# A decoder layer on one core: thresholds for each FFN matrix by itself, and all 16 tiles of FFN rows turned by transfers

## The reference

```
x = layernorm(x + latent_attention(x))         # 16 heads, 64 latent keys, softmax over the 4 largest
x = layernorm(x + cross_attention(x, ctx))     # 16 heads, low-rank keys and values from ctx, rope
x = layernorm(x + ffn(x))

# ffn, gains g1, g2, g3:
linear_bit(x, w, g) = act_quant(rmsnorm(x, g)) @ ternary(w).T
act_quant(x)        = round(x * 127 / max|x|) * max|x| / 127          # per row
ternary(w)          = round(tanh(w / s)) * arctanh(s),  s = mean|w|   # one s per matrix
h                   = silu(linear_bit(x, w1, g1)) * linear_bit(x, w2, g2)
ffn(x)              = linear_bit(h, w3, g3)                           # w1, w2: 1024 x 256, w3: 256 x 1024
```

## Time and profile before

| | us |
|---|---|
| three timed runs | 341.0, 341.74, 341.8 (median 341.74) |
| the profiled execution | 338.98 |
| its span, first to last instruction | 337.2 |
| mean granted TensorE clock | 0.993 of full speed |
| packets' data | 30.67 MB, 15.01 MB of it read from HBM |

### The profile page before, as it was taken

The page is one execution under the profiler, slowest core; times in us unless marked ns, Lnnn a source line. Parts: engine busy times, 40 slices in busy tenths (PEclk is TensorE's granted clock), DMA queues, the critical chain, the costliest instruction groups (busy, mean ns, idle before and its releaser), DMA issues.

```text
span 337.2 us, 7128 instructions
## 1 busy us (share of the span) xinstructions
PE 306.2 (91%) x2368; PEld 196.8 (58%) x2371; DVE 277.7 (82%) x704; ACT 279.7 (83%) x495; POOL 263.0 (78%) x282
## 2 busy tenths in 40 slices
PE   7788999989898979999999999999999999888882
PEld 3587678444576655564755658565757555555441
DVE  1397426999987799999998999998989999998861
ACT  2569889995468667777997979999899989999994
POOL 3265704889899994999996898999878999988641
PEclk9979999999999999999999999999999999999999
DMA  7999930005103120141030343528436235543011
GB/s 229 231 412 404 405 108 2 1 2 96 29 2 64 32 48 17 33 78 32 18 66 16 64 83 44 94 48 143 80 73 77 56 72 118 110 80 77 1 49 47
DMA packets 58292, 30.67 MB, mean 91 GB/s; under 512 B 53584, under 2 KB 56144, under 8 KB 57168
## 3 DMA queue, kind: packets, MB, share of 16 engines
q1 hardware_dynamic: 58256, 30.22, 36.7%
HBM read 15.01 MB, written 2.10 MB: 51 GB/s over the span
## 4 chain that ended last, share of the span: by engine, by line
PE 47%; ACT 16%; POOL 12%; issue 11%; DMA 7%; DVE 5%; SPq 0%; POOLq 0%; ACTq 0%; DVEq 0%
PE wide L575 10%; PE wide L607 6%; DMA region_c<-in_wkcqT 4%; PE wide L563 4%; PE wide L632 3%; POOL P L1419 3%; PE wide L538 3%; PE wide L495 3%; PE wide L531 3%; PE wide L589 2%; DMA w_raw<-w_raw 2%; ACT region_t L940 2%; PE wide L469 2%; ACT region_c L934 2%; PE wide L507 2%
## 5 line engine op out<-in xcount | busy, mean ns | idle before, releaser
L575 PE MATMUL wide<-B_sb,x1T 128*128 128x512 f32 x128 | 57.9, 597 | 0.8 <-DVE region_c L1218 0.8
L1111 DVE MAX8 m<-Ls 128x8 f32<-128x64 f32 x256 | 34.0, 209 | 14.9 <-ACT Ls L812 14.8
L607 PE MATMUL wide<-V,PT 128*128 128x256 f16 x384 | 44.7, 273 | 0.4 <-DVE V L1154 0.2
L607 PEld LDWEIGHTS wide<-V,PT 128*128 128x128 f16 x384 | 36.8, 98 | 8.9 <-issue 2.3
L1384 POOL TENSOR_TENSOR Ls<-Ls,m 128x1024 f32<-128x1024 f32 x16 | 30.9, 1932 | 10.7 <-DVE m L1111 10.7
L575 PEld LDWEIGHTS wide<-B_sb,x1T 128*128 128x128 f32 x128 | 23.6, 190 | 26.5 <-issue 24.1
L632 PE MATMUL wide<-tern,region_k 128*128 128x512 f16 x128 | 32.6, 380 | 4.1 <-ACT region_k L918 1.7
L1427 POOL TENSOR_TENSOR P<-P 128x1024 f16<-128x1024 f32 x16 | 34.2, 2135 | 1.9 <-ACT P L873 1.9
L1391 POOL TENSOR_TENSOR Ls<-Ls,masks 128x1024 f32<-128x1024 f32 x16 | 35.0, 2188 | 0.3
L1419 POOL TENSOR_TENSOR P<-P,r 128x1024 f32<-128x1024 f32 x16 | 33.5, 2095 | 1.3
L866 ACT ACTIVATE P<-P,tiny 128x1024 f32<-128x1024 f32 x16 | 18.3, 1142 | 9.1 <-DVE P L1168 6.0
(11 more groups left out here) (202 smaller groups left out, 835.8 us busy)
## 6 DMA issues: line engine op xcount, KB each, us to landing
region_q<-in_wqx SPq DMA_DIRECT2D x1, 2048.0 KB, 19.3
region_c<-in_woTx SPq DMA_DIRECT2D x1, 2048.0 KB, 10.1
out_x<-region_q SPq DMA_DIRECT2D x16, 128.0 KB, 1.9
region_c<-in_wkcqT SPq DMA_DIRECT2D x2, 768.0 KB, 13.5
region_r<-in_t1w SPq DMA_DIRECT2D x1, 1024.0 KB, 9.7
region_r<-in_w1T SPq DMA_DIRECT2D x1, 1024.0 KB, 13.0
region_t<-in_w2T SPq DMA_DIRECT2D x1, 1024.0 KB, 15.0
w_raw<-in_w3T SPq DMA_DIRECT2D x1, 1024.0 KB, 17.0
```

Source lines behind the costliest of these rows:

```text
L575: mm = pe.matmul(pair(HOME_L2, n)[:, r * 512:(r + 1) * 512], x1T[n % 2][:, k, :], B_sb[:, n // 2 % 2, k, r * 512:(r + 1) * 512], start=(k ...
L607: mm = pe.matmul(bank(HOME_O2, n)[:, 0:D], PT16[n % 2][:, u * PAIRS + c, :], V16[:, b % 2, w, c, :], start=(u == w == c == 0), stop=(u == ...
L1111: ins = dve.max(m8[n % 2][:, h, :], Ls[n % 2][:, h * L:(h + 1) * L])
```

## The change

Of the matrices' preparation: each matrix gets its own S3, thresholds and semaphore counts, in the order third, first, second (`TURN_OF = (1, 2, 0)` maps a matrix to its turn). w3T is loaded before context, w1T as soon as both T1_ have read region_r, w2T behind woTx. centre_3 is split: sum_3 stays on DVE, the eight scalings go to ACT. TURNED becomes 16, so that XQT, HT, copy_XQ and copy_HT are not called any more, and turn_x, turn_h are for all tiles. The second activation of square_2 becomes an instruction of POOL in roots_2. All HOME_ tables and the five orders are new.

```diff
-TURNED = 12
+TURNED = 16
+TURN_OF = (1, 2, 0)
...
             sp.dma_start(wv1, a["wv1"]).then_inc(ld_wv, 16)
+            sp.dma_start(w3_raw[:], a["w3T"]).then_inc(ld_raw3, 16)
             sp.dma_start(context[:], a["context"]).then_inc(ld_ctx, 16)
             sp.dma_start(xT[:, 1], a["xT"][:, 1]).then_inc(ld_x1, 16)
             sp.dma_start(wqx, a["wqx"]).then_inc(ld_wqx, 16)
             sp.dma_start(wkckv, a["wkckv"]).then_inc(ld_C, 16)
+            sp.wait_ge(p_T1, 2)
+            sp.dma_start(w_raw[0], a["w1T"]).then_inc(ld_raw1, 16)
             sp.wait_ge(p_T2, 1)
             sp.dma_start(woTx, a["woTx"]).then_inc(ld_C, 16)
+            sp.dma_start(w_raw[1], a["w2T"]).then_inc(ld_raw2, 16)
             sp.dma_start(xT[:, 2:4], a["xT"][:, 2:4]).then_inc(ld_x23, 16)
-            sp.wait_ge(p_T1, 2)
-            sp.dma_start(w_raw[0], a["w1T"]).then_inc(ld_raw1, 16)
-            sp.dma_start(w_raw[1], a["w2T"]).then_inc(ld_raw2, 16)
-            sp.dma_start(w3_raw[:], a["w3T"]).then_inc(ld_raw3, 16)
             sp.dma_start(xT[:, 4:8], a["xT"][:, 4:8]).then_inc(ld_x47, 16)
...
+            turn_high_P(15); turn_low_P(15); store(7); turn_h(10); turn_x(13); turn_x(14); store(8)
+            turn_h(11); turn_x(15); store(9); store(10); turn_h(12); turn_h(13); store(11); turn_h(14)
+            store(12); turn_h(15); store(13); store(14); store(15)
...
-            def S3(*freed):
+            def S3(w, *freed):
...
-                pe.wait_ge(c_abs, 3)
-                pe.matmul(bank(HOME_S3, 0)[:, 0:3], ones[:], prep[:, 0, :], start=True, stop=True
+                pe.wait_ge(c_abs, TURN_OF[w] + 1)
+                pe.matmul(bank(HOME_S3, TURN_OF[w])[:, 0:1], ones[:], prep[:, 0, w:w + 1], start=True, stop=True
...
+            WT(0, a_R, 1); Q(1); T2T(a_T2k, 1); RT(1, v_WF, 1); L1(2, a_Q, 2); PT1(1, v_AT, 1, a_R, 2)
+            A_(0, a_T2, 1); XW(0, a_PT1, 2); O1(0); WB(); S3(2, a_L1, 3, v_mask, 3); B_(0, 0); WT(1)
+            X1T(0, v_y1, 1); C_(0); A_(1, a_X1, 1); PT1(2, v_AT, 2, c_mean, 2); C_(1, a_B, 1)
+            XW(1, a_A, 2); O1(1); S3(0, a_C, 1); B_(1, 0, a_PT1, 3); L1(3, c_mean, 4, v_y1, 2)
...
+            def centre_3():
+                act.wait_ge(c_sum3, 1)
+                for c in range(FC):
+                    ins = act.activation(tern3[:, c, :], tern3[:, c, :], ACT.Identity, scale=-float(D),
+                                         bias=tern3_sum[:, c:c + 1])
+                ins.then_inc(c_cent, 1)
...
-                act.wait_ge(a_sq2, n + 1)
-                act.activation(parts2[n], eps_parts[:], ACT.Identity, bias=var2[n], scale=var1[n]).then_inc(a_mom2, 1)
...
-            def thresholds():
+            def thresholds(w):
+                dve.wait_ge(c_sum, TURN_OF[w] + 1)
...
-                dve.tensor_scalar(prep[:, 8, :], sums, per_weight * HALF_ATANH, RMS_EPS * HALF_ATANH,
+                dve.tensor_scalar(prep[:, 8, w:w + 1], sums, per_weight * HALF_ATANH, RMS_EPS * HALF_ATANH,
                                   ALU.mult, ALU.add).then_inc(c_thr, 1)
...
-                link(dve.tensor_reduce(tern3_sum[:], tern3[:], AX, ALU.add))
-                for c in range(FC):
-                    ins = dve.tensor_scalar(tern3[:, c, :], tern3[:, c, :], float(D), tern3_sum[:, c:c + 1],
-                                            ALU.mult, ALU.subtract)
-                ins.then_inc(c_cent, 1)
+            def sum_3():
+                dve.wait_ge(c_tern, 1)
+                dve.tensor_reduce(tern3_sum[:], tern3[:], AX, ALU.add).then_inc(c_sum3, 1)
...
-                pool.wait_ge(a_mom2, n + 1)
+                pool.wait_ge(a_sq2, n + 1)
+                pool.tensor_scalar(parts2[n], eps_parts[:], var1[n], var2[n], ALU.mult, ALU.add).then_inc(g_mom2, 1)
+                pool.wait_ge(g_mom2, n + 1)
                 pool.tensor_tensor(roots2[n], parts2[n], three_roots[:], ALU.pow).then_inc(g_rt2, 1)
```

More of the change, by code:

```diff
@@ L704, in _ @@
[L704 to L709 removed]
+            warm(9, 0); Q(0); L1(0, a_Q, 1); warm(10, 0, p_warm, 1); T1_(0); T1_(1, p_warm, 2)
@@ L996, in _ @@
-            copy_X1(8); copy_L1(12); square_3(0); square_1(8); high_P(7); pack_h(1); exp_4(11)
-            copy_PT1(11); tanh(4); square_h(3); high_V(0, 4); exp_2(8); copy_R(10); whole_x(5); exp_1(12)
-            whole_h(2); copy_X1(9); copy_L1(13); pack_x(5); exp_4(12); square_1(9); square_3(1)
-            square_h(4); pack_h(2); norm_3(0); copy_R(11); square_2(6); tanh(5); high_V(1, 4); whole_h(3)
-            copy_PT1(12); high_P(8); pack_h(3); norm_3(1); square_1(10); exp_2(9); exp_1(13); copy_X1(10)
@@ L1013, in _ @@
-            high_P(13); square_h(10); exp_2(14); square_1(15); square_2(12); tanh(11); copy_X1(15)
-            high_V(0, 7); whole_h(9); pack_h(9); high_P(14); norm_3(7); square_3(8); whole_x(12)
-            pack_x(12); high_V(1, 7); square_h(11); exp_2(15); copy_XQ(12); square_2(13); whole_h(10)
-            tanh(12); pack_h(10); norm_3(8); whole_x(13); high_P(15); pack_x(13); whole_h(11); pack_h(11)
-            square_2(14); copy_XQ(13); square_3(9); square_h(12); tanh(13); whole_x(14); square_3(10)
@@ L1018, in _ @@
[L1018 to L1022 removed]
+            spread_lat_v(); copy_Q(0); copy_L1(0); copy_T1(0); exp_4(0); copy_T1(1); copy_L1(1); exp_1(0)
@@ new lines, in _ @@
+            copy_Q(6); high_P(5); high_V(0, 3); square_h(1); copy_L1(11); centre_3(); square_1(7)
+            exp_1(10); square_2(4); tanh(2); whole_h(0); high_V(1, 3); pack_h(0); copy_X1(7); square_1(8)
+            whole_x(3); copy_R(9); exp_4(10); whole_h(1); pack_x(3); pack_h(1); exp_2(6); exp_1(11)
+            copy_PT1(10); copy_B(0, 2); copy_B(1, 2); exp_2(7); exp_4(11); copy_L1(12); square_h(2)
+            high_P(6); whole_x(4); pack_x(4); copy_R(10); tanh(3); square_3(0); copy_B(2, 2)
@@ new lines, in _ @@
+            copy_PT1(11); copy_B(3, 2); copy_L1(13); copy_X1(8); square_2(5); exp_4(12); exp_1(12)
+            tanh(4); whole_h(2); high_P(7); pack_h(2); square_h(3); square_1(9); norm_3(0); copy_X1(9)
+            copy_R(11); square_3(1); whole_x(5); square_2(6); pack_x(5); square_h(4); exp_2(8)
+            high_V(0, 4); copy_PT1(12); whole_x(6); tanh(5); copy_X1(10); high_V(1, 4); copy_Q(7)
+            exp_1(13); exp_4(13); pack_x(6); high_P(8); norm_3(1); whole_h(3); square_3(2); pack_h(3)
@@ new lines, in _ @@
+            tanh(6); square_1(10); exp_2(9); copy_PT1(13); copy_R(12); copy_L1(14); square_h(5)
+            whole_h(4); high_P(9); pack_h(4); copy_X1(11); square_1(11); square_2(7); copy_R(13)
+            norm_3(2); exp_4(14); exp_2(10); square_h(6); square_3(3); high_V(0, 5); high_V(1, 5)
+            whole_h(5); exp_1(14); square_2(8); copy_B(0, 3); norm_3(3); pack_h(5); exp_2(11); whole_x(7)
+            square_2(9); pack_x(7); high_V(0, 6); whole_x(8); copy_B(1, 3); high_P(10); copy_B(2, 3)
@@ L1513, in rope_tables @@
+            root_3(13); root_3(14); root_3(15)
 def rope_tables():
```

406 lines of the change are left out of this document (189 added, 217 removed).

## The result

The changed kernel takes 330.97 us (median of 3 runs, 327.8 to 331.4) against 341.74 before: a ratio (of the means) of 0.9664, 95% interval 0.9569 to 0.9759. The forecast was 338.4 us with a range from 334.5 to 344.5: the sign was right, the size was not. Four later comparisons, each with its kernels on one chip, gave the kernel before medians of 339.2 to 339.7 us, so some 2 us of the 341.74 are not the change's doing; in the first of them the changed kernel took 331.11, ratio 0.9705 (0.9616 to 0.9794). Either way it gains 8 to 11 us where 3.3 were forecast. The profiled executions are 338.98 and 331.38 us, 7.6 apart.

A forecast was written before the change was run, and what follows sets the result against it. It took PE as nearest the bound in the steady part and ACT in the tail. Terms -3.7 (mark), -1.1 (ACT behind it) and +1.5 (last turn) gave -3.3 us, so 338.4 us, range 334.5 to 344.5.

The forecast's parts named there:

- I take PE's 3.7 us, the bound with the least idle time, as the shift of the mark: Steady part, L2(0) to exp_2(15): the last exponential's start (the mark) comes 3.7 us earlier, by PE's moved work.
- The tail is ACT's: Stretch from exp_2(15) to the end: ACT, busy 40.74 of 45.30 us, sets its length.
- the term of -1.1: Behind exp_2(15): ACT loses 7.5 us of work and gets 6.4 moved there, so 1.1 us less.
- the 47 that I had named as the mark of an error: Stretch behind exp_2(15): the forecast is wrong if this tail is longer than 47 us.
- costs nothing: Set-up: ternary(2) and row sums moved there are covered by DVE's 17 us of idle time, costing nothing themselves.
- The loads: Set-up: 2 MB more ahead of woTx, 5.1 us; C_(0) at about 39.1, the load covered by 0.6 us.
- Rival D: Set-up: the loads' 0.6 us of cover is gone and PE waits 2.6 us; 341.0 us, chance 0.09.
- A: Ahead of exp_2(15): ACT's and DVE's relief counts in full, -7.4 us; 334.7 us, chance 0.14.
- B: Steady part: POOL becomes the bound, so exp_2(15) starts no earlier; 342.1 us, chance 0.12.
- C: Tail: DVE's backlog of 36.5 us, not ACT, ends last, up to 4.4 us longer; 343.9 us, chance 0.15.
- E: Last four tiles: transfer turns on the path of each, 1.5 us later apiece; 342.9 us, chance 0.12.
- The rule on transposes: Last h turn: TensorE advised, 390 ns a block against 1309 by transfer; end 8.6 us later, sum 345.5 us.

The follow-up runs named there:

- run 2: Kernel before, old orders, with all the change's moves of work put in at places of the author's choice; 342.81 us, ratio 1.0062 to the kernel before.
- run 1: The changed kernel timed again, unedited, as yardstick on one chip with the others; 331.11 us, ratio 0.9705 to the kernel before.
- run 14: Kernel before plus eight extra unused row sums on VectorE in front of largest_h(1); 344.21 us, ratio 1.0137 to the kernel before.
- run 9: Changed kernel plus eight extra unused row sums on VectorE in front of largest_h(0); 334.96 us, ratio 0.9844 to the kernel before.
- run 11: Changed kernel with centre_3's scalings early on VectorE, row sums right behind ternary(2); 329.98 us, ratio 0.9693 to the kernel before.
- run 15: Changed kernel with exp_2(15) moved later on ScalarE, no work added; 335.39 us, ratio 0.9884 to the kernel before.
- run 6: Changed kernel with only the last tile's h turned by TensorE and ScalarE; 328.64 us, ratio 0.9663 to the kernel before.
- run 7: Changed kernel with ternary(2) and its row sums late, behind ternary(1); 337.81 us, ratio 0.9946 to the kernel before.
- run 8: Changed kernel with centre_3's eight scalings back on VectorE, in front of largest_h(0); 339.66 us, ratio 1.0006 to the kernel before.
- run 10: Changed kernel plus eight extra unused scalings on VectorE in front of largest_h(0); 341.02 us, ratio 0.9998 to the kernel before.
- run 12: Changed kernel with square_2's three-column step back on ScalarE, off GpSimd; 331.34 us, ratio 0.9738 to the kernel before.
- run 3: Kernel before, old orders, with TURNED = 16 alone; 345.74 us, ratio 1.0154 to the kernel before.

## Why the prediction was wrong in size

- **The step that failed** is "I take PE's 3.7 us, the bound with the least idle time, as the shift of the mark". It subtracts one engine's moved work and takes its idle time of 11.7 us as fixed. The moved work was about right: PE's busy time in the steady part fell by 4.8. But the mark came 10.0 us earlier, 0.8 of it from the set-up. The rest is PE idle time, 4.4 us less, which I gave no term. About half of that came with the moves and half with the orders: with all the moves and the old orders it is 9.4 us (run 2), with the new ones 7.2 (run 1). The forecast had even named one knot, DVE on the chain of waits with the row sums at 127.18 us, and had then given its removal no price. Which steps of the new orders save the second half was not taken apart.
- **Why busy and idle time misled me.** Idle time in this kernel is no slack. 3.6 us of DVE work at one place cost 4.2 in the kernel before, where DVE sat idle for 16.8 us of the steady part (run 14), and 5.2 in the changed one (run 9). In the other direction work taken away gives little unless the order follows: 9.3 us of DVE and 3.3 of ACT for 2.8 (run 2), 3.3 us of ACT for nothing (run 11). I read this as the time of a chain that goes from engine to engine; the chain itself was followed link by link only near the end. A forecast from the moved work needed the links of the new orders, which I had read at the two marks only.
- **"The tail is ACT's"** holds up to pack_h(15), and no further. The tail of before and of the changed kernel, cut at the end of pack_h(15):

```profile
291.90:329.64 37.74, 30.24 (x208) 17.86 (x208) 31.22 (x70) 37.51 (x68) 26.09 (x25) 1.00 0.26 54
329.64:337.24 7.60, 1.66 (x16) 1.16 (x16) 0.91 (x3) 3.22 (x9) 1.08 (x2) 0.93 0.15 52
```
```profile
281.90:320.12 38.22, 31.29 (x194) 17.40 (x190) 34.59 (x78) 37.40 (x66) 30.56 (x30) 1.00 0.51 91
320.12:329.70 9.58, 3.38 (x22) 1.99 (x22) 1.61 (x5) 2.94 (x9) 1.66 (x3) 0.90 0.36 96
```

  Ahead of pack_h(15) ACT is idle for 0.2 us in the one and 0.8 in the other. But the term of -1.1 was wrong: ACT's work behind the mark fell by 0.4 (40.74 to 40.34), and the way to pack_h(15) grew by 0.5. And less work for ACT there shortens nothing by itself: run 15 took 4.4 us of it away, and ACT then stood idle. The other 2.0 of the 2.5 us by which the tail grew lie behind pack_h(15); I had put 1.5 there (1.2 to 2.6), which was right. Run 6 made the last turn shorter, and the norms behind it kept the end where it was. The sum -1.1 + 1.5 said 0.4, and 47.8 is beyond the 47 that I had named as the mark of an error.
- **ternary(2) in the set-up, "costs nothing"**: right, and too modest. Its late place in the new orders costs 7.1 us of steady part (run 7), for 8.2 us more of DVE's work there. I had given the early place no value.
- **centre_3**: on ACT 0.497 us each, 4.0 in all as forecast; as they overlap by 0.1 us, they hold ACT for 3.29 us (148.23 to 151.52). Of its absence from DVE I counted 2.3 us; at its place in the new orders it is worth 8 (runs 1 and 8): there it meets a busy GpSimd and takes 6.5 us, and the tight plan adds the rest. The trace of before had the sign: ternary's second step took 3.87 us there once and 2.35 twice. The Trainium skill (SBUF — State Buffer, Who interferes with whom) states the rule that I had missed: VectorE and GpSimd share a port pair as an exclusive lock, which VectorE takes for a tensor_scalar in one of its two-port fast modes, and for two inputs from SBUF beside a GpSimd instruction that reads SBUF, but not for tensor_reduce. By it a scaling can wait for a whole GpSimd instruction and a row sum never, which is what runs 9 and 10 show (up to 2.06 us against 0.42 at most).
- **GpSimd's new step**: 0.349 us each (16 of them), not the 0.23 that I took from "the same operation", and far from the upper end of 0.863. Run 12 shows that the choice of the engine doesn't matter here.
- **The loads**: woTx landed 12.9 us after its issue, not 10.1 + 5.1, and C_(0) started at 40.0, where I had 39.1; PE was busy 39.04 of 40.10 us of that stretch. Rival D did not happen.
- **The rivals.** A's sign, a mark before 286, came, and its 334.7 is nearest; but its mechanism, the relief of ACT and DVE counting in full, is not what the runs show: in the old orders 12.6 us of it gave 2.8 (run 2), and in the new ones 3.3 us less of ACT's work gave nothing (run 11). That its time came nearest is luck. B: GpSimd's idle time in the steady part did fall, from 23.9 to 11.7 us, and it is not the bound (run 12). C: DVE has 36.2 us of work in the tail (36.5 forecast), and ACT is idle 7.5 us there, short of the 8 that I had asked for; it does not decide. E is real in the old orders (6.5 us of tail, run 3) and mostly hidden by the new: before, PE waited 2.7 us for ACT's copies of h, in the changed kernel 3.7 for its turns.
- **The rule on transposes** (the Trainium skill, VectorE: DVE Perf Modes, The three transpose paths): the estimate from it, 10.5 us for an h tile, put the end 8.6 us later. Measured: 3.8 us for the whole step, 1.9 more than before. The direction was right, the size was not.
